# Attention with a feed-forward network beside it: rounds of one and two steps, and staggered feed-forward outputs

## The reference

```python
xn = _layernorm(x, axis=-1)
q = _rope(split(xn @ Wq + bq)); k = _rope(split(xn @ Wk + bk)); v = split(xn @ Wv + bv)   # 16 heads of 16
weights = softmax(einsum('bhnd,bhmd->bhnm', q, k) / sqrt(256))
attn = einsum('bhnm,bhmd->bhnd', weights, v).transpose(0, 2, 1, 3).reshape(b, n, 256) @ Wo + bo
h = concatenate([xn, -xn], axis=-1)
h = relu(s0 * (h @ W(k0))) * 2        # W(k) is +1 where the boolean is set, -1 elsewhere; 512 -> 1024
h = relu(s1 * (h @ W(k1))) * 2        # 1024 -> 1024
h = s2 * (h @ W(k2))                  # 1024 -> 256
out = x + attn + h
```

## Time and profile before

| | |
|---|---|
| time, median of 3 runs | 3007.37 us (3006.82 to 3008.39) |
| the profiled execution's own time | 3009.63 us |
| its span | 3007.8 us |
| TensorE busy (matmul) | 2747.8 us, 91% |
| ScalarE busy | 2098.7 us, 70% |
| VectorE busy | 1036.6 us, 34% |
| exponentials (L844) | 2048, 1938.6 us |
| weighing (L883) | 8192 instructions, 994.3 us |
| scores (L868) | 4096, 861.5 us |

### The profile page before, as it was taken

The page is one execution under the profiler, slowest core; times in us unless marked ns, Lnnn a source line. Parts: engine busy times, 40 slices in busy tenths (PEclk is TensorE's granted clock), DMA queues, the critical chain, the costliest instruction groups (busy, mean ns, idle before and its releaser), DMA issues.

```text
span 3007.8 us, 55125 instructions
## 1 busy us (share of the span) xinstructions
PE 2747.8 (91%) x20423; PEld 1337.5 (44%) x20423; DVE 1036.6 (34%) x1609; ACT 2098.7 (70%) x2301; POOL 373.4 (12%) x309
## 2 busy tenths in 40 slices
PE   6777299998989999999999999999999999999997
PEld 3444144444444444444444444444444444444444
DVE  7999422222222323222232223232322223222322
ACT  4446277776767777777777677777777777777773
POOL 5888200000000000000000000000000000000000
PEclk9889699999999999999999999999999999999998
DMA  6666411112111211212222212121222122221212
GB/s 204 196 195 189 125 42 45 41 47 55 44 39 45 70 45 49 61 50 58 54 68 54 66 42 65 44 77 45 56 56 52 53 54 68 54 68 43 71 38 95
DMA packets 279715, 212.13 MB, mean 71 GB/s; under 512 B 183616, under 2 KB 227392, under 8 KB 272960
## 3 DMA queue, kind: packets, MB, share of 16 engines
q1 hardware_dynamic: 271040, 200.30, 24.7%
q10 hardware_dynamic: 8448, 8.39, 0.9%
HBM read 132.08 MB, written 76.55 MB: 69 GB/s over the span
## 4 chain that ended last, share of the span: by engine, by line
PE 66%; issue 10%; ACT 7%; DMA 2%; SPq 2%; DVE 1%; POOL 1%; ACTq 0%; POOLq 0%; DVEq 0%
PE ps_o L883 27%; PE ps_s L868 20%; PE ps_f L928 16%; ACT probs L844 7%; PE ps_f L907 2%; SPq L762 1%; DMA y<-rest_sum_d 1%; POOL heads L997 1%; DVE sums L1018 1%; PE ps_f L978 0%; DMA q_rows<-row_shift 0%; DMA heads_t<-heads 0%; DVE h_hi L1028 0%; ACTq L843 0%; DMA probs<-rest_sum_d 0%
## 5 line engine op out<-in xcount | busy, mean ns | idle before, releaser
L844 ACT ACTIVATE probs<-ps_s 128x1024 f32<-128x1024 f32 x2048 | 1938.6, 1029 | 693.9 <-PE ps_s L868 693.6
L883 PE MATMUL ps_o<-probs,v_ones 128*32 128x512 f32 x8192 | 994.3, 603 | 0.0
L868 PE MATMUL ps_s<-q_rows,k_rows 50*128 50x512 f32 x4096 | 861.5, 460 | 126.3 <-ACT probs L844 50.1
L868 PEld LDWEIGHTS ps_s<-q_rows,k_rows 50*128 50x128 f32 x4096 | 346.7, 186 | 847.5 <-ACT probs L844 730.8
L1028 DVE TENSOR_SCALAR h_hi<-ps_f 128x512 fp32r<-128x512 f32 x256 | 175.6, 686 | 967.4 <-PE ps_f L928 967.4
L883 PEld LDWEIGHTS ps_o<-probs,v_ones 128*32 128x32 f32 x8192 | 214.7, 109 | 452.2 <-issue 307.1
L928 PE MATMUL ps_f<-h_hi,ffn_w 64*128 64x512 f32 x2048 | 405.2, 392 | 0.0
L928 PE MATMUL ps_f<-h_lo,ffn_w 64*128 64x512 f32 x2048 | 405.0, 392 | 0.0
L997 POOL TENSOR_TENSOR heads<-heads,sums 128x512 f32<-128x512 f32 x64 | 82.2, 1284 | 2261.3 <-DVE sums L1018 2261.3
L1018 DVE RECIPROCAL sums<-sums 128x128 f32<-128x128 f32 x256 | 221.0, 916 | 2.2
L928 PEld LDWEIGHTS ps_f<-h_lo,ffn_w 64*128 64x128 f32 x2048 | 193.6, 185 | 39.0
(11 more groups left out here) (87 smaller groups left out, 1364.9 us busy)
## 6 DMA issues: line engine op xcount, KB each, us to landing
k_rows<-k_parts SPq DMA_DIRECT2D x128, 256.0 KB
q_rows<-q_parts SPq DMA_DIRECT2D x384, 64.0 KB
q_parts<-parts SPq DMA_DIRECT2D x32, 512.0 KB, 3.7
k_parts<-parts SPq DMA_DIRECT2D x32, 512.0 KB, 4.6
k_rows<-k_parts SPq DMA_DIRECT2D x128, 128.0 KB
x_chunk<-in_x ACTq DMA_DIRECT2D x16, 512.0 KB, 4.2
xn_t<-xnT SPq DMA_DIRECT2D x16, 512.0 KB, 4.5
v_heads<-v_sb SPq DMA_DIRECT2D x16, 512.0 KB, 5.5
```

The costliest lines, as they stand in the source:

```text
L844: nc.scalar.activation(probs[:, s % PBUF, half * 2 * C:(half + 1) * 2 * C], ps_s[:, half].rearrange("p c n -> p (c n)"), ACT.Exp, scale=SC ...
L868: last = nc.tensor.matmul(ps_s[:, half, w], k_rows[rows, u, t * P:(t + 1) * P], q_rows[rows, u, half], start=True, stop=True)
L883: last = nc.tensor.matmul(ps_o[32 * c:32 * c + 2 * DH], v_ones[:, u, t], probs[:, s % PBUF, c * C:(c + 1) * C], start=(t == 0), stop=(t == ...
```

## The change

Line numbers of the changed kernel are 34 or 37 higher for these functions.

- **Rounds.** `ROUNDS` replaces the 32 equal cycles. A head's 16 steps are cut as 1, 2, 1, 2, ... and a last 1: eleven rounds, 44 in a pass. A round computes the scores of its steps (still two steps ahead) and weighs its steps. Rounds of two steps have three feed-forward visits (behind each of the first three halves), with weights 3, 4, 2; the last round of a head has one visit of weight 3, between scores and weighing; the other rounds of one step have none.
- **Outputs.** A layer of n outputs takes n phases. In phase p the upper rows serve output p and the lower rows output p - 1, which then is finished, so one output ends in each phase. In phase 0 the lower rows serve the last output; that partial sum is carried: VectorE copies it to `carry` (a part of `xT` or of `headsT` whose use is over) and adds it when the last output comes; in the third layer it is added to `rest` straight away. Each phase but a layer's first waits for `half_done`: 7 + 7 + 3 = 17 a pass.
- **Projection.** All eight matmuls stand together, in round 8, between its scores and its weighing.
- **SP** also waits for the first layer's outputs before it reloads `xT`.

```diff
-VISITS = {FIRST: [4, 4], PROJECT: [4, 0], SECOND: [4, 2, 4, 3, 3, 3, 4, 2, 4, 3], THIRD: [7, 4, 5, 5, 7, 4]}
+PROJECT_AT = 2 * 4
+ROUNDS = [(KT * j + t, n) for j in range(HEADS) for t, n in
+          [(3 * k + m, m + 1) for k in range(KT // 3) for m in range(2)] + [(KT - 1, 1)]]
...
+def visits():
+
+    weights = ([3, 4, 2] * (KT // 3) + [3]) * HEADS
+    counts = [[1, 2] * (FT // 2), [5] * 6 + [6] * 2, [3, 2, 3, 2]]
+    out, at = [], 0
+    for layer in (FIRST, SECOND, THIRD):
+        for phase, n in enumerate(counts[layer]):
+            share = [1, 0][:n] if layer == FIRST else weights[at:at + n]
...
                     if j == 1 and not last:
                         sp.wait_ge(xT_split, i + 1)
+                        sp.wait_ge(group_used, outs_before(i, projects) + place(projects, FIRST, FT) + 1 + BANKS)
...
+            def beside(i, projects, layer, phase, part):
+
+                at = place(projects, layer, phase)
+                size = size_of(layer)
+                if part == 0:
+
+                    out_used(i, projects, at + 1)
+                    if layer == FIRST and phase == 0:
                         pe.wait_ge(xT_split, i + 1)
...
+                    if phase > 0:
+                        pe.wait_ge(half_done, SWAPS * i + swap_number(layer, phase))
+                if phase == 0 and layer > FIRST and part in (0, 2 * (FT - 2)):
+
+                    pe.wait_ge(group_used, outs_before(i, projects) + place(projects, layer - 1, FT if part else FT - 2) + 1 + BANKS)
+                k, low = part // 2, part % 2
+                for half in range(2):
+                    n = phase if half == 0 else (phase - 1) % sums_in(layer)
+                    rows = slice(GROUP_ROWS * half, GROUP_ROWS * (half + 1))
+                    bank = ps_f[:, (at + 1 - half) % BANKS]
...
+            def project(i):
+
+                pe.wait_ge(y_loaded, 32 * i - 32 * (CB - 1))
+                for t in range(TT):
+                    at = PROJECT_PLACE + t
+                    out_used(i, True, at)
+                    for k in range(DT):
...
             def one_pass(i, projects, last=False):
...
+                for n, (first, count) in enumerate(ROUNDS):
+                    for m in range(2 * count):
+                        ahead_by = first + FFN_FROM + m // 2
+                        if ahead_by < STEPS or not last:
+                            scores(i, ahead_by, m % 2)
+                        visit = m if count == 2 else m - 1
+                        if 0 <= visit < len(VISITS[n]):
+                            for layer, phase, part in VISITS[n][visit]:
+                                beside(i, projects, layer, phase, part)
+                    if projects and n == PROJECT_AT:
+                        project(i)
+                    for m in range(count):
+                        weigh(i, first + m)
...
+            def take(i, projects, layer, n):
...
+                if n == FT - 1:
+                    dve.wait_ge(group_used, outs_before(i, projects) + place(projects, layer, 0) + 1 + BANKS)
+                    nc.vector.tensor_tensor(carry[layer], bank, carry[layer], ALU.add).then_inc(carry_added, 1)
+                    dve.wait_ge(carry_added, 2 * i + layer + 1)
+                    bank = carry[layer]
```

More of the change, by code:

```diff
@@ L99, with sums_in, size_of, spread @@
-TURNS, ENDS, ORDER = zip(*(cycles(p) for p in (False, True)))
-def groups_before(i, projects):
-    return (GROUPS + TT) * i - CB * TT if projects else GROUPS * i
+FIRST, SECOND, THIRD = range(3)
+PROJECT_AT = 2 * 4
+ROUNDS = [(KT * j + t, n) for j in range(HEADS) for t, n in
+          [(3 * k + m, m + 1) for k in range(KT // 3) for m in range(2)] + [(KT - 1, 1)]]
+def sums_in(layer):
+    return (FT, FT, TT)[layer]
+def size_of(layer):
+    return (2 * DT, 2 * FT, 2 * FT)[layer]
+def spread(total, weights):
+    ends = [round(total * sum(weights[:n + 1]) / sum(weights)) for n in range(len(weights))]
+    return [e - b for b, e in zip([0] + ends, ends)]
@@ new lines, in visits @@
+def visits():
[5 more added lines that the diff above has]
+            share = [1, 0][:n] if layer == FIRST else weights[at:at + n]
+            part = 0
+            for count in spread(size_of(layer), share):
+                out.append([(layer, phase, part + m) for m in range(count)])
+                part += count
+            at += n
+    assert len(out) == len(weights)
+    return out
@@ new lines, in rounds, with place @@
+def rounds():
+    left, out, ends = visits(), [], []
+    for at, (first, count) in enumerate(ROUNDS):
+        n = 3 if count == 2 else 1 if first % KT == KT - 1 else 0
+        out.append(left[:n])
+        ends.append([(layer, phase) for visit in left[:n] for layer, phase, part in visit if part == size_of(layer) - 1])
+        left = left[n:]
+    assert not left
+    return out, ends
+VISITS, ENDS = rounds()
+def place(projects, layer, phase):
+    if layer == FIRST:
+        return phase
+    return (FT + 1) * layer + phase + (TT if projects else 0)
@@ L107, in ahead, with swap_number, outs_before @@
+PROJECT_PLACE = FT + 1
+OUTS = (place(False, THIRD, TT) + 1, place(True, THIRD, TT) + 1)
+def swap_number(layer, phase):
+    return (FT - 1) * layer + phase
+SWAPS = swap_number(THIRD, TT - 1)
+def outs_before(i, projects):
+    return OUTS[True] * i - CB * TT if projects else OUTS[False] * i
 def ahead(b, r, n):
@@ L934, in one_pass, with out_used @@
[L934 to L951 removed]
+            def out_used(i, projects, at):
+                pe.wait_ge(group_used, outs_before(i, projects) + max(at + 1, BANKS))
@@ L1044, in split, with take_projected @@
+            def take_projected(i):
+                dve.wait_ge(y_loaded, 32 * i - 32 * (CB - 1))
+                for t in range(TT):
+                    at = PROJECT_PLACE + t
+                    dve.wait_ge(group_done, outs_before(i, True) + at + 1)
+                    nc.vector.tensor_tensor(y[:, t], ps_f[:, at % BANKS, 0:D], y[:, t], ALU.add).then_inc(group_used, 1)
             def split(i):
```

172 lines of the change are left out of this document (61 added, 111 removed).

## The result

| | before | after |
|---|---|---|
| time, median (4 runs each) | 3007.1 us (3001.98 to 3008.39) | 2857.0 us (2854.0 to 2861.7) |
| the profiled execution: own time, span | 3009.63, 3007.8 us | 2858.66, 2856.9 us |
| one pass without projection (two passes read) | 168.30, 168.28 us | 154.56, 154.05 us |
| one pass with projection (mean of nine) | 162.62 us | 154.54 us |

The ratio is 0.9505, with an interval of 0.9487 to 0.9523. The change takes off 150 us; 126 were forecast. One run of one experiment (3308.88 us, at a granted clock of 0.744) fell into a slower state of the chip and is left out of its median.

A forecast was written before the change was run, and what follows sets the result against it. A chain of latencies bounds the kernel, no engine being full; ScalarE runs dry once a cycle. Gains 4 x 10.2 + 12 x 7.0 = 124.8, less 9, plus 10, give 126: 2882 us, range 2850 to 2915 (0.6).

The forecast's parts named there:

- The chain and the short weighing: ScalarE and TensorE: latencies sum to 4.89 us a cycle before; weighing a single step, not in the trace, taken as 1.00.
- B: Round of one step ahead of each two-step round, 20 a pass: only scores and weighing, 0.67 + 1.00 = 1.67 us.
- A: Round of two steps with feed-forward visits, 20 a pass: 5.05 us, where chain and TensorE limits meet at nine pairs.
- Rival 1: Short weighing blocks on TensorE cost the upper bound, 1.43 for 1.00: 165 us more, 3047 us; chance 0.07 near its bound.
- The projection: All eight matmuls in one B, between scores and weighing: 3.64 us, hidden by nothing; pass 151.3, gain 7.0 in 12 passes.
- rival 2: TensorE becomes the bound, small waits add 0.1 on each of 44 rounds: 70 us, 2952; chance 0.2, milder and full forms.
- rival 3: Swaps and tenth pairs vanish in slack of B and A: 142.8 a pass, 5 less, 2802 us; chance 0.1.
- rival 5: No effect: the projection block stops ScalarE longer than rounds give back, costing 10 us a pass, not 3.6; chance 0.03.
- Two signs that the prediction named as wrong: In the profile after: ScalarE dry after B too, and waits for half_done over 0.3 us.
- the wait for y: TensorE's projection waits for y and heads, 10.0 us, and this goes since it comes some 7 us later in a pass.
- the end of the body: TensorE's gap at a loop body's end (2.5 us) and the 1.2 GHz stretch behind it stay: the same loops.
- Rival 4: TensorE's clock: one more low-clock stretch in each pass costs 1.0, 16 us: 2898, inside the range; no separate chance given.

The follow-up runs named there:

- straight-line kernel: The changed kernel with all 16 passes written out one after the other on TensorE, other engines keeping their loops: 2826.1 us, ratio 0.9407.

## Why the prediction was right, and where it was 24 us short

**The chain and the short weighing: right.** TensorE's loads in two rounds of the kernel after, answering to the earlier trace rows:

```profile
1558.83 0.30 PEld L905 LDWEIGHTS ps_s<-q_rows,k_rows 50*128 50x128 f32 x4 [0.84 <-ACT probs L881]
...
1559.49 0.16 PEld L920 LDWEIGHTS ps_o<-probs,v_ones 128*32 128x32 f32 x8 [0.36 <-issue]
1560.52 0.19 PEld L905 LDWEIGHTS ps_s<-q_rows,k_rows 50*128 50x128 f32 x2 [0.88 <-ACT probs L881]
...
1565.56 0.30 PEld L905 LDWEIGHTS ps_s<-q_rows,k_rows 50*128 50x128 f32 x4 [0.84 <-ACT probs L881]
```

B is 1.69 (1558.83 to 1560.52; worked out 1.67), A 5.04 (5.05), both 6.73 (6.72). The short weighing is 1.03 here, because the next scores wait 0.04 for an exponential, and 1.00 where they don't. Rival 1, with 1.43, is out. The rule of the Trainium skill (TensorEngine Tiling, Key Properties) that a change of tiling mode drains TensorE is not contradicted: two changes fit into the 0.14 of a block that no set accounts for. It did not decide here.

**The projection: right.** Loads of the round with it, answering to the earlier trace rows:

```profile
1619.75 0.30 PEld L905 LDWEIGHTS ps_s<-q_rows,k_rows 50*128 50x128 f32 x4 [0.84 <-ACT probs L881]
1620.42 3.32 PEld L968 LDWEIGHTS ps_f<-wo,headsT 128*128 128x128 f32 x16 [0.36 <-issue]
1624.07 0.16 PEld L920 LDWEIGHTS ps_o<-probs,v_ones 128*32 128x32 f32 x8 [0.33 <-issue]
1625.06 0.19 PEld L905 LDWEIGHTS ps_s<-q_rows,k_rows 50*128 50x128 f32 x2 [0.84 <-issue]
```

5.31, as worked out (1.67 + 3.64), and with half of the matmuls left out 1.58 a pass went.

**The copy at a head's start: right.** 45 waits, three in each of 15 passes. At the one near 1552 the boundary is at 1552.05 and the weighing loads at 1552.93, 0.88 later for 0.69: 0.19 each, where 0.2 was taken.

**The pass as a whole: right where no loop end lies in it.** In the straight-line kernel a pass is 152.54 with projection. Worked out were 151.3 and three copy waits of 0.2, so 151.9. Without projection, by ScalarE at the same place of two passes, 148.98 for 148.3:

```profile
509.38 1.94 ACT L881 ACTIVATE probs<-ps_s 128x1024 f32<-128x1024 f32 x2 [1.34 <-PE ps_s L905]
...
658.36 1.94 ACT L881 ACTIVATE probs<-ps_s 128x1024 f32<-128x1024 f32 x2 [1.34 <-PE ps_s L905]
```

Some 0.7 over in both; with projection 0.5 of it is not there in the changed kernel's own pass without a jump ahead (152.06). So rival 2 (0.1 more on each round, 4.4 a pass) did not come, nor did rival 3 (142.8 a pass), nor rival 5. Two signs that the prediction named as wrong were there in part: in rounds other than the plain one ScalarE is dry between as well, for 0.2 to 0.4 us (the 0.26 at 1576.95), and the longest wait for a swap is 0.4 us, with a mean of 0.24 where 0.20 was taken. The pass came out as worked out all the same.

**Three terms of the sum were mis-sized**, and they can be told apart on ScalarE, by the starts of its exponentials in the two profiled executions. There the gain is 150.9 us (spans), 25.1 more than the sum's 125.8.

| us, in all 16 passes | before | after | taken |
|---|---|---|---|
| cycles at the lower clock behind empty visits | 7.7 | 0 | 0 |
| cycles with the projection's first half (the wait for y), over 5.11 each | 15.0 | 0 | 10 before, 0 after |
| 13 jumps back, over the worked-out passes (157.9 and 158.35; 148.3 and 151.9) | 56.1 | 42.9 | the same in both |
| of them, each of the 3 behind a pass without projection | 7.9 | 5.9 | 3.5 |
| of them, each of the 10 between passes with projection | 3.2 | 2.5 | 3.5 |

The first three rows give 7.7, 5.0 and 13.2 us that the sum had not: 25.9, which is the 25.1 to within 1 us.

- *The empty cycles.* The sum of before, 4 x 5.15 + 28 x 4.905, priced them like the others, and the clock as full. I had checked it, and the clock, only in a pass with projection. With 3.5 for the end of the body it gives 161.4, and the passes are 168.3. Of these 6.9, the slow cycles are 3.3 in one pass and 1.6 in the other. Rival 4 had the right mechanism and the wrong sign: the change took a stretch at the lower clock away.
- *The wait for y.* It was put at the 10.0 us of the list of waits. With the slow matmuls behind it, it cost 15.0.
- *The end of the body*, "the same loops", was put at no difference, and this is the largest of the three. At the jump behind the pass at 530.24, the kernel before has a last cycle of 8.58 and a first of 9.64, for 4.905 and 5.15:

```profile
685.77 3.77 ACT L844 ACTIVATE probs<-ps_s 128x1024 f32<-128x1024 f32 x4 [1.12 <-PE ps_s L868]
694.35 1.94 ACT L844 ACTIVATE probs<-ps_s 128x1024 f32<-128x1024 f32 x2 [4.81 <-PE ps_s L868]
...
703.99 1.94 ACT L844 ACTIVATE probs<-ps_s 128x1024 f32<-128x1024 f32 x2 [2.37 <-PE ps_s L868]
```

For the first two an experiment shows the direction: filling the empty cycles gave 10.5 us, and moving the wait away gave 20, each with shorter loop ends besides. For the third there is only the count of one execution of each kernel. Why the same jump costs less in the changed kernel, and more behind a pass without projection in both, is open. So half of the 25 us lie in a term whose mechanism isn't known.

One pass without projection of the kernel after, and TensorE's loads at its end:

```profile
518.36:672.92 154.56, 151.71 (x1218) 71.82 (x1218) 46.93 (x71) 122.22 (x129) 7.91 (x8) 0.97 0.19 49
```

```profile
663.74 0.16 PEld L920 LDWEIGHTS ps_o<-probs,v_ones 128*32 128x32 f32 x8
666.76 0.31 PEld L905 LDWEIGHTS ps_s<-q_rows,k_rows 50*128 50x128 f32 x4 [2.86 <-issue]
667.71 0.18 PEld L920 LDWEIGHTS ps_o<-probs,v_ones 128*32 128x32 f32 x4 [0.65 <-issue]
670.15 0.19 PEld L920 LDWEIGHTS ps_o<-probs,v_ones 128*32 128x32 f32 x4 [2.25 <-issue]
672.00 0.28 PEld L905 LDWEIGHTS ps_s<-q_rows,k_rows 50*128 50x128 f32 x2 [1.67 <-issue]
```

The first weighing of the next pass takes 4.3 us there for 1.0 (667.71 to 672.00), released by nothing that the profile shows, and the granted clock of 668.36 to 673.36 is 0.50. Why one loop's end costs more than the other's was not tried.

## What to carry to other kernels

Where one engine's work and another's alternate over a buffer that holds one step, count how often the other engine runs dry for each step of work, and cut the rounds so that the short one hides behind the long block; both the number and the order matter, and the gain ends where the first engine has no slack. Check the sum against every kind of pass, those with empty places too, before the change is priced. And before a gap on an engine is removed, look which transfer is due soon behind it: the gap may be covering a wait that comes back in full. Nor does a term cancel because the code is the same on both sides: the loop end, left out of the difference as "the same loops", was half of what the forecast missed.

## What the runs showed of the hardware

- A jump back at the end of a hardware loop's body on TensorE costs 2.65 us here (21.2 us for 8 jumps), with the lower clock behind it; leaving the loop without a jump shows no gap. The Trainium skill (Runtime: NRT & Kernel Launch, Instruction fetch mechanics) says that a taken branch to a target out of the current window waits for a fetch, and that full unrolling is preferred for it. The runs agree in the changed kernel: two passes in a body and straight-line code are both faster. No run shows that the gap is a fetch. The straight line has small waits of its own (161, up to 0.8 us).
- TensorE's clock fell from 2.4 to 1.2 GHz inside a pass, in a cycle where it stood still for 0.97 and 0.42 us, behind another of the same kind; a weighing of 1.92 us then took 3.39. An empty place in a schedule can cost more than its idle time.
- A weighing block of one step takes 1.00 us, with two changes of tiling in it, and one of two steps 1.86: cutting the blocks shorter costs 0.14 each.
